# Last batch through the dense experts, the first three grouped with room for four steps of expert tiles

## The chip, the cores and the metric

One core of a Trainium2 chip runs the whole program. The metric is the device time of one execution in microseconds, taken as the median of several runs. All engine spans below come from one profiled execution.

## What is computed

Two layers over `x` of 4 batches, 256 tokens and 256 features, with a context of 4 x 256 x 64 beside it. Layer 0 builds an adjacency from the context (two projections, similarity, the top 76 of 256 in each row, a sigmoid, symmetrised), adds it and runs a gated feed-forward network with block-quantised operands. Layer 1 is an attention of 16 heads on low-rank keys, and then a mixture of 32 experts in which every token goes to one expert. The part that the change touches is that last one:

```python
logits = x4 @ router_w.T                     # 256 tokens, 32 experts
p = softmax(logits); e = argmax(p)           # one expert a token, weight p[e]
w_e = ternary(weight) * expert_masks[e]      # 256 x 256, values -1, 0, 1
out = x3 + p[e] * scale * (x4 @ w_e.T)       # x4 = layernorm(x3)
```

## The kernel before

The four batches are pipelined. In the pass of batch b the attention of batch b runs over eight head pairs p = 0 to 7. Beside it run the first layer of batch b + 1 (adjacency, top-k, feed-forward) and the experts of batch b - 1. The order on TensorE is a list written out by hand: `tensor_order()` places steps at four slots of a pair, `moe[p][0]` to `moe[p][3]`. Slot 0 stands after the key projections, slots 1 and 2 around `attn_turn(b, p, 0)` and the feed-forward steps, slot 3 just before `attn_turn(b, p, 1)`, and behind that come the scores of the next pair. The other engines walk the same list. PSUM has one large bank (QB) and six of 128x512 (S0, S1, QC, TP, GA, UA). A bank's `filled` and `drained` semaphores are counted over its turns in that list. S0 and S1 serve the scores and the experts, GA and UA the first layer.

The experts are *grouped*. `routing` finds each token's expert. `rank` and `tiles` (VectorE and TensorE) sort the tokens into 40 tiles of 32 slots, each tile belonging to one expert, and write the 40 expert numbers to `et`. `gather` (6 steps) permutes the tokens into the slots by matmuls with a 0/1 matrix, drained by ScalarE. `group` g (5 steps) multiplies 8 tiles by their 8 expert matrices: 32 matmuls into one bank (S0 for even g, S1 for odd g), drained by ScalarE into `osort[g % 2]`. The expert matrices lie as 8-bit floats in HBM (`wE_d`, 32 x 64 KB, written early in the program). `load_tiles(b, g)` fetches 8 of them, each with an address read from `et`, so SyncE executes 8 loads of 64 KB with a register load ahead of each. `wtile` holds two steps of 8 tiles, so the loads of step n wait until step n - 2 was multiplied. `store_sorted(b, g)` writes `osort` to HBM, `unsort(b)` on GpSimd fetches the 256 token rows back by an indirect DMA, and `result(b)` scales them, weights them and adds `x3`.

SyncE's queue is in order. Ahead of the first `load_tiles` stand the loads of x and context for batches 2 and 3. After that each batch is `load_tiles(0)`, `load_tiles(1)`, then `load_tiles(g)` and `store_sorted(g - 2)` in turn, the last two stores, and the store of the result. ScalarE drains `group` g only when the store of the step that used the same `osort` half has landed.

For the last batch nothing runs beside: after the attention of batch 3 the program goes through `att_out(3)`, the fourth layer norm, `moe_turn(3)`, `logits(3)`, `rank`, `tiles`, six gathers, five groups, `unsort` and `result`.

## Time and profile before

| | us |
|---|---|
| median of 3 runs | 685.72 (678.52 to 688.59) |
| the profiled execution | 686.24 |
| its span, first to last instruction | 684.4 |
| mean granted TensorE clock | 0.873 of 2.4 GHz |
| TensorE busy in the span | 501.1 (73%) |
| VectorE, ScalarE, GpSimd busy | 359.9, 228.3, 247.9 |

Busy time is the sum of an engine's own instructions. Start times in the rows below are counted from the first instruction of the span. A matmul's listed length is longer than its pitch, since successive ones overlap; the distance between two starts gives the pace.

### The profile page before, as it was taken

The numbers are of one execution on the slowest core, as the hardware profiler recorded it, in microseconds if no ns is written. First come the engines' busy times: TensorE is split into PE (matmuls) and PEld (weight loads), VectorE is DVE, ScalarE is ACT, GpSimd is POOL, SyncE is SP. The second block draws the span as 40 slices with busy tenths as digits, with TensorE's granted clock in tenths as the row PEclk, the third lists the DMA queues.
The fourth block names the chain that finished last, engine by engine and source line by source line (L and its number), as shares of the span: only waits on it lengthen the run. The fifth ranks groups of instructions, "written<-read, shape, count | busy, mean of one in ns | idle before, by whom it ended". The sixth has DMA issues, their size and how long they took to land.

```text
span 684.4 us, 9759 instructions
## 1 busy us (share of the span) xinstructions
PE 501.1 (73%) x3284; PEld 328.0 (48%) x3284; DVE 359.9 (53%) x711; ACT 228.3 (33%) x610; POOL 247.9 (36%) x258
## 2 busy tenths in 40 slices
PE   2863675877887698799987978998798986565211
PEld 1752244545445465555565645556475553351100
DVE  3999692587687238965643696476226321002000
ACT  1843121333323314363432336334114642303000
POOL 3765442368458512321344314123403220340003
PEclk9976898989999789999999999999799997866555
DMA  7941000034204300012310001121000212201222
GB/s 286 363 160 61 1 0 4 1 113 155 79 22 133 97 2 18 1 56 73 95 32 16 0 10 55 49 73 51 31 1 5 59 47 74 66 15 39 74 82 68
DMA packets 44416, 43.93 MB, mean 64 GB/s; under 512 B 7888, under 2 KB 40528, under 8 KB 43472
## 3 DMA queue, kind: packets, MB, share of 16 engines
q1 hardware_dynamic: 43984, 42.27, 19.3%
q0 software_dynamic: 384, 1.05, 0.5%
q8 instruction: 26, 0.43, 0.3%
q14 instruction: 22, 0.18, 0.1%
HBM read 34.92 MB, written 8.39 MB: 63 GB/s over the span
## 4 chain that ended last, share of the span: by engine, by line
PE 36%; DVE 26%; issue 11%; POOL 9%; SPq 7%; ACT 7%; DMA 2%; POOLq 0%; DVEq 0%; ACTq 0%
PE qc L560 9%; PE qb L560 8%; PE ga L560 6%; PE s L560 5%; SPq L521 4%; PE ua L560 3%; SPq L523 3%; PE tp L563 3%; DVE wk L1147 3%; POOL reg L1458 2%; DVE top L1145 2%; DVE amax L1072 2%; ACT reg L942 2%; POOL wst L1506 2%; DVE reg L1219 2%
## 5 line engine op out<-in xcount | busy, mean ns | idle before, releaser
L1458 POOL TENSOR_TENSOR reg<-reg,rsum 128x512 f32<-128x512 f32 x64 | 68.9, 1096 | 177.0 <-DVE rsum L1233 177.0
L942 ACT ACTIVATE reg<-s,nmax 128x256 f32<-128x256 f32 x128 | 58.9, 476 | 47.2 <-DVE nmax L1226 47.1
L560 PE MATMUL qc<-reg,wM 128*64 128x256 f32 (+1 forms) x384 | 71.1, 409 | 4.5 <-DVE reg L1219 2.8
L560 PE MATMUL qb<-reg,wA_hi 128*128 128x256 f16 x384 | 71.0, 291 | 2.7 <-ACT reg L927 2.7
L563 PE MATMUL tp<-idn,reg 128*128 128x128 f32 x248 | 43.9, 304 | 38.6 <-POOL reg L1458 21.6
L1226 DVE TENSOR_REDUCE nmax<-s 128x2 f32<-128x512 f32 x64 | 40.9, 680 | 34.6 <-PE s L560 34.6
L864 ACT COPY reg<-tp 128x512 f32<-128x512 f32 (+1 forms) x56 | 32.0, 571 | 81.1 <-PE tp L563 81.1
L1219 DVE TENSOR_TENSOR reg<-qb,cosq 128x768 f32<-128x768 f32 x32 | 30.5, 954 | 51.5 <-PE qb L560 51.5
L560 PE MATMUL s<-wtile,moe 128*32 128x256 fp8e4 x640 | 26.2, 317 | 42.0 <-DMA wtile<-wE_d 41.5
L563 PEld LDWEIGHTS tp<-idn,reg 128*128 128x128 f32 x248 | 30.9, 153 | 52.9 <-POOL reg L1458 28.1
L560 PEld LDWEIGHTS qc<-reg,wM 128*64 128x64 f32 (+1 forms) x384 | 38.2, 158 | 34.3 <-issue 22.2
L560 PEld LDWEIGHTS qb<-reg,wA_hi 128*128 128x128 f16 x384 | 36.2, 103 | 23.4 <-issue 12.7
L1506 POOL TENSOR_TENSOR wst<-masks,tern 128x512 fp8e4<-128x512 f32 x32 | 45.0, 1435 | 5.2 <-DMA masks<-in_moe_masks 5.2
L560 PEld LDWEIGHTS s<-wtile,moe 128*32 128x32 f16 x640 | 18.3, 109 | 49.1 <-issue 46.8
L560 PE MATMUL qb<-reg 128*64 128x256 f32 x256 | 37.3, 412 | 5.7 <-ACT reg L864 2.9
L560 PE MATMUL s<-reg 64*128 64x256 f32 x256 | 39.2, 427 | 1.8 <-ACT moe L864 1.5
L560 PE MATMUL qb<-reg,wA_lo 128*128 128x256 f16 x192 | 39.7, 291 | 0.0
L560 PE MATMUL ga<-wG,ffn 128*128 128x512 f32 x64 | 32.7, 636 | 9.5 <-DVE sg L1182 8.8
L560 PE MATMUL ga<-wD,ffn 128*128 128x256 f32 x128 | 34.5, 430 | 2.4 <-ACT ffn L864 2.4
L1389 POOL TENSOR_TENSOR ffn<-ffn,qsc 128x1024 f32<-128x1024 f32 (+1 forms) x12 | 19.5, 1623 | 42.1 <-DVE ffn L1096 42.1
L1384 POOL TENSOR_SCALAR small<-small 128x2 f32<-128x2 f32 x32 | 7.4, 232 | 68.3 <-DVE small L1122 66.5
L864 ACT COPY reg<-qb 128x256 f32<-128x256 f32 x32 | 11.9, 372 | 58.7 <-PE qb L560 58.7
(191 smaller groups left out, 959.8 us busy)
## 6 DMA issues: line engine op xcount, KB each, us to landing
wtile<-wE_d SPq DMA_DIRECT2D x160, 64.0 KB, 1.7
masks<-in_moe_masks SPq DMA_DIRECT2D x16, 512.0 KB, 3.7
y_d<-masks SPq DMA_DIRECT2D x20, 256.0 KB, 2.3
wM<-in_att_wq SPq DMA_DIRECT2D x1, 2048.0 KB, 8.5
moe<-in_wo_t SPq DMA_DIRECT2D x1, 2048.0 KB, 12.8
wE_d<-wst SPq DMA_DIRECT2D x16, 128.0 KB, 1.9
reg<-in_kc_q SPq DMA_DIRECT2D x1, 1536.0 KB, 11.7
reg<-in_qr_t SPq DMA_DIRECT2D x1, 1536.0 KB, 19.6
```

Of the source, the lines that this page charges most:

```text
L521: e = sp.value_load(et[0:1, 8 * g + i:8 * g + i + 1], min_val=0, max_val=E - 1)
L523: sp.dma_start(wtile[:, o:o + P], wE_d[bass.ds(e, 1)].rearrange("o p x -> p (o x)")).then_inc(ld_w[n % 2].sem, 16)
L560: return nc.tensor.matmul(dst, lhsT, rhs, start=start, stop=stop, skip_group_check=not check)
L563: return nc.tensor.transpose(dst, src, idn[:, :])
L864: nc.scalar.copy(dst, src).then_inc(bank.drained, 1)
L942: nc.scalar.activation(attn[p % 2][:, k * S:(k + 1) * S], s.tensor[:, (k % 2) * S:(k % 2 + 1) * S], ACT.Exp, bias=nmax[:, o:o + 1], accum_ ...
L1147: nc.vector.match_replace(wk[:, t * S:(t + 1) * S], best, cur, -3.0e38).then_inc(topk_step.sem, 1)
L1219: nc.vector.tensor_tensor(qcs[:, g * J * S:(g + 1) * J * S], QB.tensor[:, 0:J * S], tab[:, :], ALU.mult).then_inc(qc_ready.sem if g == 0 e ...
L1226: nc.vector.tensor_reduce(nmax[:, o:o + 2], v3(k.tensor[:, :], T), AX_X, ALU.max, negate=True).then_inc(nmax_ready.sem, 1)
L1389: nc.gpsimd.tensor_tensor(v3(dst, blocks), v3(src, blocks), scale.unsqueeze(2).to_broadcast([P, blocks, BLK]), ALU.mult).then_inc(ready.se ...
L1458: nc.gpsimd.tensor_tensor(a, a, rsum[:, o + 2 * hh:o + 2 * hh + 2].unsqueeze(2).to_broadcast([P, 2, S]), ALU.mult).then_inc(attn_ready.sem, 1)
L1506: last = nc.gpsimd.tensor_tensor(we[:, :, c, :], src[:, c], tern[:, c * D:(c + 1) * D].unsqueeze(1).to_broadcast([P, EC, D]), ALU.mult, sa ...
```

## The change

The last batch gets a *dense* form. All 32 expert matrices (2 MB) are fetched by one DMA into the space of the feed-forward weights `wG` and `wU`. Every token half t (0, 1) is multiplied by all 32 matrices: 16 fills of two banks, each bank two experts wide (128x512), even fills in GA and UA for tokens 0 to 127, odd ones in S0 and S1 for tokens 128 to 255. `selw` is the routing weight where the expert is the token's own, and 0 elsewhere. ScalarE drains the first half with a scale by `selw` (two instructions a bank) and GpSimd adds the drained rows up. VectorE drains the second half with a multiply-add straight from PSUM (two instructions a bank). At the end each path adds its two partial sums, multiplies by `scale` and adds `x3`, and each half is stored by its own DMA. The tokens are split in a high and a low 16-bit part from the transposed `x4T`, by ScalarE and VectorE, no longer by GpSimd.

For batches 0 to 2 `wtile` holds four steps of tiles instead of two; all five `load_tiles` of a batch are queued ahead of all five stores; the loads of x and context for batch 3 move behind the fourth `load_tiles` of batch 0; gathers and groups move to other slots; `unsort` moves behind the last `rstd` of the pass. The four new functions `expert` stand in the order TensorE, ScalarE, VectorE, GpSimd in the diff. To make room, `qm` now shares `sim` and `wk`, `wst` lies in `moe`, and the raw `wo` passes through `wtile`.

```diff
-    steps += [("att_out", B - 1), ("moe_turn", B - 1), ("logits", B - 1), ("rank", B - 1), ("tiles", B - 1)]
-    steps += [("gather", B - 1, i) for i in range(GATHERS)]
-    steps += [("group", B - 1, g) for g in range(GROUPS)]
+    steps += [("att_out", B - 1), ("moe_turn", B - 1), ("logits", B - 1)]
+    steps += [("expert", B - 1, f) for f in range(FILLS)]
...
-    ([("gather", 0)], [], [("gather", 1)], [("gather", 2)]),
-    ([("gather", 3)], [], [("gather", 4)], [("gather", 5)]),
-    ([("group", 0)], [], [("group", 1)], []),
-    ([("group", 2)], [], [("group", 3)], []),
-    ([("group", 4)], [], [], []),
+    ([], [("gather", 0)], [("gather", 1)], [("gather", 2)]),
+    ([("gather", 3)], [("gather", 4)], [], [("gather", 5)]),
+    ([], [], [], [("group", 0)]),
+    ([("group", 1)], [], [], [("group", 2)]),
+    ([("group", 3)], [], [], [("group", 4)]),
...
-                if n >= 2:
-                    key = ("group", (n - 2) // GROUPS, (n - 2) % GROUPS)
+                if n >= RING:
+                    key = ("group", (n - RING) // GROUPS, (n - RING) % GROUPS)
...
-            for b in range(2, B):
-                load_a(b)
-                load_b(b)
-            for b in range(B):
-                load_tiles(b, 0)
-                for g in range(1, GROUPS):
+            load_a(2)
+            load_b(2)
+            for b in range(B - 1):
+                for g in range(GROUPS):
                     load_tiles(b, g)
-                    if g >= 2:
-                        store_sorted(b, g - 2)
-                store_sorted(b, GROUPS - 2)
-                store_sorted(b, GROUPS - 1)
+                    if g == RING - 1 and b + 3 < B:
+                        load_a(b + 3)
+                        load_b(b + 3)
+                for g in range(GROUPS):
+                    store_sorted(b, g)
+                if b == B - 2:
+                    key = ("ffn_up", B - 1, 3)
+                    for k in both_banks(*key):
+                        sp.wait_ge(k.filled, k.done(key))
+                    sp.dma_start(v3(wE.bitcast(F32), E), wE_d[:, :, :].rearrange("e p x -> p e x")).then_inc(ld_dense.sem, 16)
...
+            def expert(b, f):
+                q, t = divmod(f, T)
...
+                for half, k in enumerate(both_banks("expert", b, f)):
+                    e = EF * q + 2 * half
+                    pe.wait_ge(k.drained, k.free(("expert", b, f)))
+                    for c in range(C):
+                        for i, src in enumerate((xhi, xlo)):
+                            last = mm(v3(k.tensor[:, :], 2), src[:, c * S + t * P:c * S + (t + 1) * P], w[:, e:e + 2, c, :],
+                                      c == 0 and i == 0, c == C - 1 and i == 1)
+                    last.then_inc(k.filled, 1)
...
+            def expert(m):
+                for half, k in enumerate(both_banks(*key)):
+                    n = 2 * m + half
+                    act.wait_ge(k.filled, k.done(key))
...
+                    if n > 2:
+                        act.wait_ge(summed.sem, n - 2)
+                    for i in range(2):
+                        e = EF * m + 2 * half + i
+                        dst = acc[:, 0, i] if n == 0 else scaled[half][:, i * D:(i + 1) * D]
+                        ins = nc.scalar.activation(dst, k.tensor[:, i * D:(i + 1) * D], ACT.Copy, scale=selw[:, 0, e:e + 1])
+                    ins.then_inc(k.drained, 1)
...
+            def expert(m):
+                for i in range(EF):
+                    e, chain, k = EF * m + i, i % 2, banks[i // 2]
+                    src, w = k.tensor[:, chain * D:(chain + 1) * D], selw[:, t, e:e + 1]
...
+                        ins = nc.vector.scalar_tensor_tensor(acc[:, t, chain], src, w, acc[:, t, chain], ALU.mult, ALU.add)
+                    ins.then_inc(acc_step.sem if chain == 0 else k.drained, 1)
...
+            def expert(m):
+                for half, k in enumerate(both_banks(*key)):
+                    n = 2 * m + half
+                    pool.wait_ge(k.drained, k.done(key))
+                    if n > 1:
+                        pool.wait_ge(summed.sem, n - 1)
+                    if n > 0:
+                        nc.gpsimd.tensor_tensor(acc_rows[:, 0:2 * D], acc_rows[:, 0:2 * D], scaled[half], ALU.add)\
+                            .then_inc(summed.sem, 1)
...
-                    if p == PAIRS - 1 and b >= 1:
-                        unsort(b - 1)
...
                 if b >= 1:
+                    unsort(b - 1)
                     result(b - 1)
```

## Rows read from the trace of the kernel before

**Rows 1.** Page of the profile, part 2: TensorE and its clock in 40 slices

```profile
PE   2863675877887698799987978998798986565211
PEclk9976898989999789999999999999799997866555
```

**Rows 2.** Timeline of the end: start, length, instruction, count, idle before and its cause

```profile
614.07 1.91 PE L560 MATMUL qc<-rtr,moe 128*128 128x32 f32 x8 [0.68 <-ACT moe L864]
616.02 0.23 DVE L1251 TENSOR_REDUCE small<-qc 128x2 f32<-128x64 f32 x1 [6.70 <-PE qc L560]
617.44 0.17 DVE L1264 RECIPROCAL small<-small 128x2 f32<-128x2 f32 x1
...
621.10 25.82 SPq L523 DMA_DIRECT2D wtile<-wE_d  x24
...
667.24 1.90 PE L560 MATMUL s<-wtile,moe 128*32 128x256 fp8e4 x32 [7.27 <-DMA wtile<-wE_d]
...
676.94 1.26 POOL L1490 TENSOR_TENSOR tern<-tern,scl 128x512 f32<-128x512 f32 x1 [1.78 <-DMA tern<-y_d,slot_u]
...
681.52 0.38 SPq L553 DMA_DIRECT2D out<-tern  x1
```

**Rows 3.** Busy time by stretch: stretch, length, busy of each engine, clock, DMA share, GB/s

```profile
624.00:628.00 4.00, 3.74 (x14) 0.80 (x14) 0.00 (x0) 3.59 (x8) 0.00 (x0) 1.00 0.19 55
628.00:684.00 56.00, 9.49 (x160) 6.29 (x160) 0.00 (x0) 3.42 (x6) 6.40 (x6) 0.52 0.24 74
```

**Rows 4.** Timeline of batch 3's attention, where batch 2 is grouped

```profile
527.88 0.18 DVE L1305 TENSOR_SCALAR et<-qc 1x40 int32<-1x40 f32 x1
...
528.78 33.67 SPq L523 DMA_DIRECT2D wtile<-wE_d  x24
...
554.18 8.27 SPq L523 DMA_DIRECT2D wtile<-wE_d  x8
...
563.72 8.30 SPq L523 DMA_DIRECT2D wtile<-wE_d  x8
...
573.59 1.90 PE L560 MATMUL s<-wtile,moe 128*32 128x256 fp8e4 x32 [6.71 <-DMA wtile<-wE_d]
...
576.46 2.08 PE L560 MATMUL s<-reg 64*128 64x256 f32 x8
```

**Rows 5.** DMA issues: size of each, median us from issue to landing

```profile
y_d<-masks SPq DMA_DIRECT2D x20, 256.0 KB, 2.3
wM<-in_att_wq SPq DMA_DIRECT2D x1, 2048.0 KB, 8.5
```

**Rows 6.** Timeline, matmul pace at 2.4 GHz (two pairs), weight load at 1.2 GHz

```profile
531.87 0.53 PE L560 MATMUL s<-moe,xhi 128*128 128x432 f16 x2
532.23 0.53 PE L560 MATMUL s<-moe,xlo 128*128 128x432 f16 x2
...
620.60 0.15 PEld L560 LDWEIGHTS s<-moe,xlo 128*128 128x128 f16 x1 [0.21 <-issue]
```

**Rows 7.** Timeline, prices of the drains and adds

```profile
550.44 0.47 ACT L942 ACTIVATE reg<-s,nmax 128x256 f32<-128x256 f32 x1
550.89 0.48 ACT L942 ACTIVATE reg<-s,nmax 128x256 f32<-128x256 f32 x1
...
359.53 0.42 DVE L1196 TENSOR_TENSOR x<-y,ga 128x256 f32<-128x256 f32 x1 [7.00 <-PE ga L560]
...
678.30 1.84 POOL L1493 TENSOR_SCALAR tern<-tern,small 128x256 f32<-128x256 f32 x2
680.23 1.26 POOL L1495 TENSOR_TENSOR tern<-tern,reg 128x512 f32<-128x512 f32 x1
...
213.97 7.81 POOL L1506 TENSOR_TENSOR wst<-masks,tern 128x512 fp8e4<-128x512 f32 x4
```

**Rows 8.** Timeline of batches 1 and 2, around the groups and `result`

```profile
442.45 0.44 SPq L528 DMA_DIRECT2D y_d<-masks  x1
...
455.57 1.06 PE L560 MATMUL s<-wtile,moe 128*32 128x256 fp8e4 x32
...
362.47 0.20 POOL L1409 TENSOR_TENSOR small<-small 128x2 f32<-128x2 f32 x1
...
374.55 1.50 POOL L1384 TENSOR_SCALAR th<-th 128x512 f32<-128x512 f32 x1 [7.37 <-ACT th L908]
```

More of the change, by code:

```diff
@@ L30 @@
 NEC = E // EC
+EF = 4
 G = 32
+RING = 4
 NT = 40
@@ L224, in banks_of @@
         return [("GA", "UA")[args[1] % 2]]
+    if name == "expert":
+        return ("GA", "UA") if args[1] % T == 0 else ("S0", "S1")
     if name == "group":
@@ L294, in build @@
         top = sb("top", T * 8)
-        ffn = sb("ffn", 6144)
-        hid, qy, qm, hq = (ffn[:, i * I:(i + 1) * I] for i in range(4))
-        hqT = ffn[:, 4096:5120]
-        xn = ffn[:, 5120:5632]
-        xqT = ffn[:, 5632:6144]
+        ffn = sb("ffn", 5120)
+        hid, qy, hq = (ffn[:, i * I:(i + 1) * I] for i in range(3))
+        qm = simwk[:, :]
+        hqT = ffn[:, 3072:4096]
+        xn = ffn[:, 4096:4608]
+        xqT = ffn[:, 4608:5120]
+        acc = ffn[:, 0:T * 2 * D].rearrange("p (t k d) -> p t k d", t=T, k=2)
+        acc_rows = ffn[:, 0:T * 2 * D]
+        scaled = [ffn[:, 1024:1536], ffn[:, 1536:2048]]
+        selw = v3(ffn[:, 2048:2048 + T * E], T)
         sg = sb("sg", 512)
@@ L396, in build @@
         st_w = [count(f"st_w{i}", 0, 16 * NEC // 2) for i in range(2)]
-        ld_w = [count(f"ld_w{i}", 0) for i in range(2)]
-        st_y = [count(f"st_y{i}", 16 * (GROUPS + 1 - i) // 2 if i == 0 else 16 * (GROUPS // 2)) for i in range(2)]
+        ld_w = [count(f"ld_w{i}", 0) for i in range(RING)]
+        ld_dense = count("ld_dense", 0, 16)
+        st_y = [count(f"st_y{i}", 16 * ((GROUPS + 1 - i) // 2)) for i in range(2)]
         ld_y = count("ld_y", 16 * T)
@@ L853, in _ @@
                 keys_turn, x_turn, project_first, project, to_keys, scores, attn_turn, context, att_out, moe_turn, logits, rank, tiles,
-                gather, group)}
+                gather, group, expert)}
             for name, *args in order:
@@ L952, in moe_turn @@
                 drain(TP, ("moe_turn", b), x4T, TP.tensor[:, :])
+                if b == B - 1:
+                    act.wait_ge(TP.drained, TP.done(("moe_turn", b)))
+                    nc.scalar.copy(xhi[:, :], x4T).then_inc(xsplit_ready.sem, 1)
             def route_exp(b):
@@ L961, in gather @@
                 c, (o, w) = i // len(PIECES), PIECES[i % len(PIECES)]
+                if b == 0 and i == 0:
+                    for q in st_w:
+                        act.wait_ge(q.sem, q.setup)
                 for h, k in enumerate(both_banks(*key)):
@@ L972, in group @@
                 drain(bank_of("group", b, g), ("group", b, g), osort[g % 2], bank_of("group", b, g).tensor[:, :])
+            def expert(m):
+                key = ("expert", B - 1, T * m)
+                for half, k in enumerate(both_banks(*key)):
+                    n = 2 * m + half
+                    act.wait_ge(k.filled, k.done(key))
+                    if m == 0 and half == 0:
+                        act.wait_ge(rt_step.sem, rt_step.at(B - 1, 6))
+                    if n > 2:
[5 more added lines that the diff above has]
+                    ins.then_inc(k.drained, 1)
             def moe_step(b, name, *args):
@@ L1057, in _ @@
             route_exp(B - 1)
-            for i in range(GATHERS):
-                gather(B - 1, i)
-            for g in range(GROUPS):
-                group(B - 1, g)
+            for m in range(FILLS // T):
+                expert(m)
         @block.vector
@@ L1375, in _ @@
             routing(B - 1)
-            rank(B - 1)
-            tiles(B - 1)
+            dve.wait_ge(rt_step.sem, rt_step.at(B - 1, 6))
+            for m in range(FILLS // T):
+                expert(m)
+            o, last = acc[:, 1, 0], ("expert", B - 1, FILLS - 1)
+            k = both_banks(*last)[1]
+            dve.wait_ge(k.drained, k.done(last))
+            dve.wait_ge(acc_step.sem, 2 * FILLS // T)
+            nc.vector.tensor_tensor(o, o, acc[:, 1, 1], ALU.add).then_inc(last_step.sem, 1)
+            dve.wait_ge(last_step.sem, 1)
+            nc.vector.tensor_tensor(o, o, scl[:, :], ALU.mult).then_inc(last_step.sem, 1)
+            dve.wait_ge(last_step.sem, 2)
+            nc.vector.tensor_tensor(o, o, x3[:, D:2 * D], ALU.add).then_inc(last_step.sem, 1)
         @block.gpsimd
@@ L1565, in _ @@
                 if b >= 1:
+                    unsort(b - 1)
                     result(b - 1)
             rstd(B - 1, 3)
-            split(B - 1)
-            unsort(B - 1)
-            result(B - 1)
+            for m in range(FILLS // T):
+                expert(m)
+            o, last = acc[:, 0, 0], ("expert", B - 1, FILLS - T)
+            k = both_banks(*last)[1]
+            pool.wait_ge(k.drained, k.done(last))
+            pool.wait_ge(summed.sem, FILLS - 1)
+            nc.gpsimd.tensor_tensor(o, o, acc[:, 0, 1], ALU.add).then_inc(osum.sem, 1)
+            pool.wait_ge(osum.sem, 1)
+            nc.gpsimd.tensor_tensor(o, o, scl[:, :], ALU.mult).then_inc(half_step.sem, 1)
+            pool.wait_ge(half_step.sem, 1)
+            nc.gpsimd.tensor_tensor(o, o, x3[:, 0:D], ALU.add).then_inc(o_ready.sem, 1)
 def tables():
```

85 lines of the change are left out of this document (65 added, 20 removed).

## The prediction, made before the changed kernel was run

> **What bounds the kernel now.** I read the page's slices first [rows 1]: TensorE is busy in 60 to 99% of most slices at nearly full clock, until slice 34; in the last four it is busy in 10 to 20%, at half clock. The end is therefore a stretch with another limit, and the timeline of the end says which [rows 2]. The logits of the last batch are done at 616.0, and the span ends at 684.4: 68.4 us for the experts of one batch. In that time SyncE issues 40 loads of 64 KB; 24 of them take 25.82 us, so one step of 8 costs 8.6 us of issue, and each group of TensorE work (1.90 us) waits for them, the last one for 7.27 us. The windows confirm it [rows 3]: of 56 us TensorE works 9.5, all other engines less, and the DMA engines are only 24% busy. What is late is SyncE's issue of dynamic loads, not bandwidth and not arithmetic. Behind it come the sort's store, the indirect fetch, and `result`.
>
> The same limit shows once more in the attention of batch 3, which has nothing of a next batch to fill it [rows 4]. `et` of batch 2 is written at 527.9, SyncE starts at 528.8, but the third step of loads starts only at 554.2, when group 0 has freed its half of `wtile`. Group 3 then waits 6.71 us for its tiles, and the scores of pair 6 start at 576.46, half clock by then.
>
> **Part 1, the dense last batch.** Counted from 616.0.
>
> TensorE: 16 fills x 2 banks x 4 matmuls = 128 matmuls of 512 columns. At the full clock two matmuls of 432 columns start 0.36 us apart from the next two [rows 6], 0.42 ns a column, so 0.213 us for 512. The trace has no 8-bit operand on the full array, only the groups' 32-column tiles; I allow up to 8% over the pace, 0.23 us. With 0.221: 28.3 us (27.3 to 29.4). The clock is at 1.2 GHz when the logits end. After comparable starts it rose inside a few us, and in the gathers it stayed at 1.00 although each step waited for a drain [rows 3]. I take 3 us of work at half clock, 1.5 us lost (0 to 3). TensorE ends at 616.0 + 28.3 + 1.5 = 645.8.
>
> Do the drains keep up? At full clock a step of four banks takes TensorE 3.5 us. ScalarE has four instructions in it; the pitch of its 128x256 reads from PSUM with a per-row operand is 0.45 us [rows 7], so 1.8 us. VectorE has four, a 128x256 from PSUM costs 0.42 [rows 7]: 1.7 us. GpSimd has two adds of 128x512 at 1.26 plus 0.08 [rows 7]: 2.7 us. Each is under 3.5, and a bank has three other fills' time for its drain. `selw` is ready at about 617.9 (the reciprocal at 617.44 [rows 2] and one small product); the first bank is full at about 617.8, so nothing waits. The split of `x4T` lies beside the logits. `rank`, `tiles`, gathers, groups, the store and the indirect fetch go.
>
> After TensorE's end: the last bank of the first half is full two fills earlier, 644.0; ScalarE is done with it at 645.1; GpSimd's last two adds end at 646.8; its three closing operations on 128x256 cost about 0.65 each by half of the 1.26 (one row has 0.92 for a scaled 256 [rows 7], an upper end), with gaps 2.2: 649.0. VectorE closes at about 648.2. Two stores are issued, the second at 649.5. From the issue of the result's store to the end of the span it is 684.4 - 681.52 = 2.9 us now [rows 2], so the span would end at 652.4. From the logits on: 36.4 us instead of 68.4, a gain of 32.0.
>
> The dense load of 2 MB must be there by 616. SyncE reaches it behind the last store of batch 2, about 585. A load of this size from HBM took 8.5 us [rows 5], in longer rows; by the 74 GB/s at 24% of the engines [rows 3], which is about 310 GB/s for this mix at full share, it takes 7 us. Even 20 us would be covered by the 30 in between. It runs beside the indirect fetch of batch 2, whose `result` ended 4 us ahead of its reader; I cost it at nothing, 0 to 3 us if the fetch queues behind it.
>
> **Part 2, batch 3's attention.** With room for four steps, loads 0 to 3 need no group, and load 4 only group 0, long done. SyncE issues all five in a row: 528.8 + 5 x 8.6 = 571.8. So no group waits for tiles: group 2 stands at slot 3 of pair 5, about 564.5, with its tiles there since 556. But the stores now stand behind all loads. Store 0 is issued at 571.8 and lands 2.3 us later [rows 5] at 574.3, and ScalarE may drain group 2 (same half of `osort`) only then. Behind that drain in ScalarE's queue stand the turned attention and the next pair; and S0 is held, which the scores of pair 6 need. So the wait of 6.71 us for tiles is replaced by one of about 8.5 us for a store. Scores of pair 6: 574.3 + 0.1 + 0.58 for the drain = 575.1, against 576.46. The pair that follows keeps its length less the small wait of the old group 4, and holds one group more, in slots with slack. Gain 1.3 us (0.5 to 2.5).
>
> **Part 3, batches 1 and 2.** The moves take groups out of the path before the scores of pair 6 (three stand there instead of four, 1.0 us each [rows 8]), and add two hand-overs of S0 just ahead of scores, about 0.25 each. I take 0.5 us gain a batch, 1.0 in all (from -1 to 2). The same store wait is covered here: in batch 2 the first three steps end at 442.4 [rows 8] after a start at 407, so load 4 follows group 0 (at about 442.5) and ends near 451; store 0 has landed by 453.5, and group 2 stands behind the last `ffn_up`, near 458: 4 to 5 us to spare. `unsort` moved behind `rstd` makes `result` end about 5 us later, near 372 in batch 1; GpSimd's next work starts at 374.55 [rows 8], so it hides, with 2 to 3 us of cover. The later load of batch 3's inputs is not read for some 40 us more. The shared buffers add no wait: the same engine uses them in order.
>
> **Sum.** 32.0 + 1.3 + 1.0 = 34.3 us. The profiled execution took 686.24, of which 684.4 is the span, and that lies 0.5 over the median: 651.9 by the profiled run, 651.4 by the median. Forecast 652, its own range 646 to 658: 1.5 for the pace of the matmuls, 1.5 for the clock, 2 for the parts 2 and 3, and the runs themselves, which spread from 678.5 to 688.6.
>
> **Rivals.**
> (a) *GpSimd bounds the dense stretch.* Its four products of 128x512 at 213.97 took 7.81 us beside VectorE work, 1.95 each instead of 1.26 [rows 7]. With 2.02 a step, 15 adds from 620.5 end at 650.8, the closing operations at 654, the span at 657.5: 657. For it: VectorE works all through. Against it: it reads one operand from PSUM, as it did in many stretches where GpSimd kept its pace. 0.12. The Trainium skill ("VectorE: DVE Perf Modes", section "Two Vector instructions with no wait between them") has the second SBUF read shared with GpSimd for Vector instructions of two SBUF tensors or in a two-port mode; by that rule the new multiply-add leaves GpSimd alone and this case falls away.
> (b) *TensorE does not keep its clock.* The fills go round four banks and each waits for a drain; if the gaps bring the clock down again for half of the stretch, 128 matmuls take 28.3 x 1.5 = 42 us and the time is 664; at 1.2 GHz throughout, 55 us, 677. The tail of the groups did run at 0.52 [rows 3], but with waits of 7 us; the gathers, with waits of 0.4, kept 1.00. 0.10. The Trainium skill ("TensorE: Matmul & The Clock Gate", section "A second HAM failure mode: psum-queue depth-cycling") reports just this for matmuls of 512 columns that cycle through PSUM banks. By that rule the time is near 664; by the gathers' row, 652.
> (c) *The wait for the store does not form*, because SyncE gets through its five steps sooner or group 2 comes later. Then all of the old wait goes: scores of pair 6 near 567, 643.5. Against it: both 8.6 us a step and the position of the store are plain. 0.10.
> (d) *Slower.* Each expert matmul stays at 1.2 GHz and shows its weight load: 0.427 + 0.15 [rows 6] = 0.577 us, 128 of them 73.9 us, the end at 616.0 + 73.9 + 6.6 less 2.3 = 694, a time of 696. It decides from (68.4 - 6.6 + 2.3) / 128 = 0.50 us a matmul. Against it: weight loads lay beside matmuls everywhere in the trace. 0.03.
>
> **How the numbers follow.** Forecast 0.65, (a) 0.12, (b) 0.10, (c) 0.10, (d) 0.03. The range reaches into (c) and to the first form of (b): 643 to 665. A measurement of this kernel tells about 2% from no change, 13.7 us: under 672 is faster. That is all but the full form of (b) and (d): faster 0.92, same 0.05, slower 0.03.
>
> **What would show it.** Right: no run of 40 tile loads at the end; about 30 us between the logits and TensorE's last matmul at a granted clock near 1.00, spacing 0.21 to 0.23; GpSimd finishing last; in batch 3 no group waiting for tiles, but ScalarE idle some 8 us before the third drain into `osort`, released by the landing of a store. Wrong: a clock of 0.5 to 0.8 in the stretch, GpSimd's adds longer than 1.7 us, TensorE waiting for the dense load, `att_out` of batch 3 late behind `result`, or a new wait in batches 1 and 2 at group 2.

## The result, and the profile after

The changed kernel takes 653.00 us (median of 4 runs, 652.87 to 654.12); the kernel before, taken on the same chip among them, 683.14 (4 runs, 678.52 to 688.59). The ratio is 0.956, with a 95% interval of 0.948 to 0.964. The profiled execution took 652.87 us with a span of 651.1, against 686.24 and 684.4: 33.3 us less.

The page's slices of the kernel after, TensorE and its granted clock in tenths, answer to [rows 1]:

```profile
PE   2871875868897689789997797899968989666696
PEclk9987699797999879989999898999987999976799
```

Where the kernel before was busy in 10 to 20% of its last three slices at half clock, there is now one slice busy to 90% or more and one to 60%, since TensorE ends at 644.7 of 651.1 us, both at nearly full clock. The slices cannot give the size, so all traces of this study are cut at three marks, which every kernel here has: `et` of batch 2 is written; VectorE's first reduction over the logits of batch 3 starts; the span ends.

| execution | `et` of batch 0 at | `et(0)` to `et(2)` | `et(2)` to logits | logits to end | span |
|---|---|---|---|---|---|
| before | 281.8 | 246.1 | 88.1 | 68.4 | 684.4 |
| after | 280.9 | 246.1 | 87.9 | 36.2 | 651.1 |

Of 33.3 us, 32.2 lie in the last stretch, 0.2 in batch 3's attention, none in batches 1 and 2, and 0.9 in the first pass, which the change leaves alone. That last number is within the spread of executions: in the twelve profiled ones of this study the first pass ends anywhere from 277.5 to 283.0. So times of whole executions are not compared to a microsecond here; the stretches are.

The end, in the timeline of the kernel after (start, length, engine, line, operation, idle time before and its releaser), answers to [rows 2]:

```profile
612.90 1.92 PE L590 MATMUL qc<-rtr,moe 128*128 128x32 f32 x8 [0.68 <-ACT moe L909]
...
614.63 0.61 PE L590 MATMUL ga<-wGU,xhi 128*128 128x512 fp8e4 x1
...
614.86 0.23 DVE L1319 TENSOR_REDUCE small<-qc 128x2 f32<-128x64 f32 x1 [0.64 <-PE qc L590]
...
618.88 0.59 PE L590 MATMUL s<-wGU,xhi 128*128 128x512 fp8e4 x1
...
619.30 0.38 PE L590 MATMUL s<-wGU,xlo 128*128 128x512 fp8e4 x1
...
619.52 0.38 PE L590 MATMUL s<-wGU,xhi 128*128 128x512 fp8e4 x1
...
643.08 2.67 POOL L1617 TENSOR_TENSOR ffn<-ffn 128x512 f32<-128x512 f32 x2 [0.77 <-ACT ffn L1038]
...
644.34 0.38 PE L590 MATMUL s<-wGU,xlo 128*128 128x512 fp8e4 x1
...
645.89 0.78 POOL L1696 TENSOR_TENSOR ffn<-ffn 128x256 f32<-128x256 f32 x1
...
648.42 0.35 SPq L580 DMA_DIRECT2D out<-ffn  x1
648.82 0.43 SPq L582 DMA_DIRECT2D out<-ffn  x1
```

The first eleven expert matmuls start 0.425 us apart, at 1.2 GHz; from 619.30 on the distance is 0.216. None waits. GpSimd's three closing operations take 0.78 us each; only the first is shown. The windows give the stretch as a whole (busy time and instructions of each engine, granted clock, DMA share, GB/s), where [rows 3] showed TensorE 9.5 us busy in 56:

```profile
614.60:644.60 30.00, 30.00 (x130) 13.00 (x129) 14.44 (x38) 13.67 (x33) 17.84 (x15) 0.92 0.00 1
```

TensorE is the only engine without a gap; GpSimd, the next, works 17.8 of 30 us. Batch 3's attention, which answers to [rows 4]:

```profile
527.88 43.72 SPq L543 DMA_DIRECT2D wtile<-wE_d  x40
...
562.49 1.06 PE L590 MATMUL s<-wtile,moe 128*32 128x256 fp8e4 x32
...
571.63 13.40 SPq L549 DMA_DIRECT2D y_d<-masks  x5
...
573.95 0.58 ACT L909 COPY masks<-s 128x512 f32<-128x512 f32 x1 [10.77 <-DMA y_d<-masks]
...
574.63 2.08 PE L590 MATMUL s<-reg 64*128 64x256 f32 x8 [10.50 <-issue]
...
585.25 0.82 SPq L576 DMA_DIRECT2D wGU<-wE_d  x1
...
598.09 1.26 POOL L1601 TENSOR_TENSOR tern<-tern,scl 128x512 f32<-128x512 f32 x1 [3.97 <-DMA tern<-y_d,slot_u]
```

All 40 loads go out in one piece of 43.7 us (1.09 each). Group 2 is computed at 562.5 to 563.5, and ScalarE then stands 10.77 us before its drain, until store 0, issued behind the last load, has landed. The scores of pair 6, whose bank that drain frees, start at 574.63: the "issue" before them is this wait seen from TensorE.

### The profile page after: what moved, and what is told of

It is laid out like the page before. It is cut to its first block, busy times and chain, and to the rows that moved or that the text cites. A ratio compares the mean times of both kernels' runs of the same rounds, so it can differ in the third digit from the quotient of the medians.

```text
span 651.1 us, 9473 instructions
## 1 busy us (share of the span) xinstructions
PE 508.7 (78%) x3221; PEld 329.7 (51%) x3221; DVE 376.3 (58%) x737; ACT 232.3 (36%) x626; POOL 261.7 (40%) x268
## 4 chain that ended last, share of the span: by engine, by line
PE 45%; DVE 24%; issue 11%; POOL 9%; ACT 8%; DMA 1%; SPq 0%; POOLq 0%; DVEq 0%; ACTq 0%
PE qc L590 11%; PE qb L590 10%; PE ga L590 8%; PE s L590 8%; PE ua L590 4%; PE tp L593 3%; DVE simwk L1212 3%; POOL reg L1569 2%; DVE top L1210 2%; ACT moe L909 2%; POOL moe L1629 2%; ACT reg L987 2%; DVE reg L1284 2%; DVE amax L1137 1%; DVE small L1184 1%
## 5 line engine op out<-in xcount | busy, mean ns | idle before, releaser
L987 ACT ACTIVATE reg<-s,nmax 128x256 f32<-128x256 f32 x128 | 58.9, 476 | 44.0 <-DVE nmax L1291 43.7
L1629 POOL TENSOR_TENSOR moe<-masks,tern 128x512 fp8e4<-128x512 f32 x32 | 45.5, 1449 | 5.2 <-DMA masks<-in_moe_masks 5.2
L590 PE MATMUL ga<-wGU,ffn 128*128 128x512 f32 x64 | 32.5, 632 | 8.5 <-DVE sg L1247 7.3
L590 PEld LDWEIGHTS s<-reg 64*128 64x128 f32 x256 | 24.6, 198 | 21.9 <-issue 20.8
L590 PE MATMUL ga<-wD,ffn 128*128 128x256 f32 x128 | 32.3, 410 | 2.4 <-ACT ffn L909 2.4
L590 PE MATMUL qc<-wF,reg 128*128 128x256 f32 x128 | 31.2, 407 | 0.5 <-ACT reg L909 0.5
```

Of the source, the lines that this page charges most:

```text
L590: return nc.tensor.matmul(dst, lhsT, rhs, start=start, stop=stop, skip_group_check=not check)
L987: nc.scalar.activation(attn[p % 2][:, k * S:(k + 1) * S], s.tensor[:, (k % 2) * S:(k % 2 + 1) * S], ACT.Exp, bias=nmax[:, o:o + 1], accum_ ...
L1629: last = nc.gpsimd.tensor_tensor(we[:, :, c, :], src[:, c], tern[:, c * D:(c + 1) * D].unsqueeze(1).to_broadcast([P, EC, D]), ALU.mult, sa ...
```

## The experiments

The theory on record: the dense end gives the gain, bounded by TensorE; the new queue order gives nearly nothing, because a wait for tiles turned into a wait for a store; GpSimd and the clock are near, but not bounds. The stretches below are those of this table: one profiled execution of each kernel. Where nothing was edited they repeat to 0.1 us from `et(2)` to the logits (87.9 to 88.0) and to 0.6 us in the dense end (35.6 to 36.2), but from `et(0)` to `et(2)` they spread by 11 us. The extra adds, the extra matmuls, the moved group 4 and the two together ran on one chip, the others on another, so their medians are compared by the ratio to the kernel before on the same chip.

| execution | `et(0)` at | to `et(2)` | to logits | to end | span | median | ratio to before |
|---|---|---|---|---|---|---|---|
| dense end alone | 278.7 | 244.9 | 87.7 | 36.0 | 647.4 | 652.08 | 0.953 (0.948 to 0.959) |
| ring and order alone | 277.5 | 247.8 | 88.0 | 69.1 | 682.4 | 686.25 | 1.004 (1.000 to 1.008) |
| store 0 ahead | 282.0 | 246.1 | 78.9 | 35.6 | 642.6 | 644.91 | 0.942 (0.937 to 0.947) |
| without low part | 281.8 | 246.1 | 87.9 | 30.0 | 645.8 | 647.56, one run | |
| 16 extra VectorE adds | 280.7 | 252.8 | 88.0 | 38.4 | 659.8 | 661.56, one run | |
| extra matmuls | 282.7 | 245.8 | 86.8 | 34.3 | 649.6 | 650.64 | 0.955 (0.950 to 0.960) |
| stores between, group 4 moved | 278.5 | 245.6 | 75.3 | 35.9 | 635.2 | 637.36 | 0.934 (0.929 to 0.938) |
| the two together | 278.3 | 241.5 | 74.9 | 35.7 | 630.3 | 635.22 | 0.931 (0.927 to 0.935) |
| and early dense load | 280.1 | 242.6 | 71.6 | 36.0 | 630.3 | 633.14 | 0.922 (0.916 to 0.929) |
| early dense load alone | 283.0 | 247.9 | 88.0 | 36.2 | 655.0 | 653.42 | 0.951 (0.946 to 0.956) |

**Dense end alone.** The changed kernel with two steps of tiles, the old queue and the old slots.

```diff
-RING = 4
+RING = 2
...
             for b in range(B - 1):
-                for g in range(GROUPS):
+                load_tiles(b, 0)
+                for g in range(1, GROUPS):
                     load_tiles(b, g)
...
-                for g in range(GROUPS):
-                    store_sorted(b, g)
+                    if g >= 2:
+                        store_sorted(b, g - 2)
+                store_sorted(b, GROUPS - 2)
+                store_sorted(b, GROUPS - 1)
```

> The dense last batch alone: two steps of tiles in the ring, the old order of SyncE's queue and the old slots of gathers and groups; the load of all matrices stays behind the stores of batch 2. Theory (the dense end is nearly the whole gain, the other two parts give 1 us together): 654 to 656, the end from the logits unchanged at 36.2 us, the old waits for tiles in batch 3 back. Rival (the new ring and order are worth several us): 658 or more.

Measured: 652.08 (649.23 to 655.92), 36.0 us from the logits to the end. The waits of TensorE for tiles are back in batch 3 (three, 8.1 us together, the longest 5.1), and that stretch still has 87.7 us against 87.9. The whole gain that these runs can tell is in this part of the change; the other gains nothing in that stretch, where 1 to 2 us were expected, and this kernel's median is even 0.9 us under that of the changed one.

**Ring and order alone.** Four steps of room, all loads ahead of all stores, the new slots, and the last batch grouped.

```diff
-    steps += [("att_out", B - 1), ("moe_turn", B - 1), ("logits", B - 1)]
-    steps += [("expert", B - 1, f) for f in range(FILLS)]
+    steps += [("att_out", B - 1), ("moe_turn", B - 1), ("logits", B - 1), ("rank", B - 1), ("tiles", B - 1)]
+    steps += [("gather", B - 1, i) for i in range(GATHERS)]
+    steps += [("group", B - 1, g) for g in range(GROUPS)]
...
```

> The new ring, queue order and slots alone, the last batch grouped again as before. Theory: 683 to 686 by the profiled span, that is the kernel before less 1 to 2 us, since SyncE's 40 loads at 1.08 us bound the end whatever the room: from the logits to the end 66 to 71 us; the stores behind all loads may add up to 2 us there. Rival (room in the ring speeds up the grouped end, because loads no longer wait for groups): 5 or more us less than before.

Measured: 686.25 (10 runs), ratio 1.0042 with an interval just above one. The 1 to 2 us did not come. At the end all 40 loads stand ahead of the first store here too. Two of the last groups still wait for their tiles, since SyncE's issue of 43.6 us bounds them whatever the room, and the last one waits for a ScalarE drain that stands behind the store (TensorE rows of this kernel):

```profile
645.74 1.90 PE L578 MATMUL s<-wtile,moe 128*32 128x256 fp8e4 x32 [6.77 <-DMA wtile<-wE_d]
654.97 1.90 PE L578 MATMUL s<-wtile,moe 128*32 128x256 fp8e4 x32 [7.33 <-DMA wtile<-wE_d]
665.00 1.90 PE L578 MATMUL s<-wtile,moe 128*32 128x256 fp8e4 x32 [8.13 <-ACT masks L897]
```

**Store 0 ahead.** One line moved in SyncE's queue of the changed kernel: the store of step 0 before the fifth step of loads.

```diff
-                    if g == RING - 1 and b + 3 < B:
-                        load_a(b + 3)
-                        load_b(b + 3)
-                for g in range(GROUPS):
+                    if g == RING - 1:
+                        if b + 3 < B:
+                            load_a(b + 3)
+                            load_b(b + 3)
+                        store_sorted(b, 0)
+                for g in range(1, GROUPS):
                     store_sorted(b, g)
```

> The changed kernel, with the store of step 0 queued ahead of the fifth step of tile loads instead of behind it. Theory (the wait of 10.77 us in batch 3 is SyncE's order): the store is issued at about 563, as soon as the fourth step of loads is out, and lands near 565.2; ScalarE waits about 2 us instead of 10.8, the scores of pair 6 start near 566 instead of 574.6, and the time is 8 to 9 us less than 653, about 644.5. Rival (something else in that pair is late just behind it, such as the fifth step of tiles): group 4 then waits for its tiles, whose loads end near 572.5 in either order, and no more than 2 to 4 us are gained, 650.

Measured: from `et(2)` to the logits 78.9 us instead of 87.9, time 644.91. ScalarE's drains of the groups in the timeline of this kernel:

```profile
566.72 0.58 ACT L911 COPY masks<-s 128x512 f32<-128x512 f32 x1 [2.43 <-DMA y_d<-masks]
...
575.94 0.58 ACT L911 COPY masks<-s 128x512 f32<-128x512 f32 x1 [3.80 <-DMA y_d<-masks]
```

10.77 us of waiting became 2.43. The store behind the loads was worth 9 us of critical path: that is shown. Against the kernel with two steps of room (87.7 us), the room and the new slots pay 8.8 us with the store moved and nothing without it; no run parts the room from the slots.

**Without the low part.** Left out: the product with `xlo`, so TensorE has 64 of 128 matmuls and the result only the f16 precision of `x4`.

```diff
-                        for i, src in enumerate((xhi, xlo)):
+                        for i, src in enumerate((xhi,)):
                             last = mm(v3(k.tensor[:, :], 2), src[:, c * S + t * P:c * S + (t + 1) * P], w[:, e:e + 2, c, :],
-                                      c == 0 and i == 0, c == C - 1 and i == 1)
+                                      c == 0 and i == 0, c == C - 1 and i == 0)
```

> The changed kernel without the low 16-bit part of the tokens in the dense matmuls, so 64 matmuls instead of 128 (this part of the result is left out). Theory (TensorE bounds the dense stretch, GpSimd comes next with 15 adds at 1.34 us): TensorE's own 27.6 us halve, but GpSimd's adds then follow one another and the stretch shrinks by only 6 to 8 us, 645 to 647. Rival (TensorE alone counts): 13 to 14 us less, 639. Rival (GpSimd or a drain bounds it already): no more than 2 us less, 651.

Measured, in one execution: the end 30.0 us instead of 36.2. GpSimd's rows now are one nearly unbroken run, 1.40 a step of addition:

```profile
619.47 1.27 POOL L1617 TENSOR_TENSOR ffn<-ffn 128x512 f32<-128x512 f32 x1 [8.63 <-ACT ffn L1038]
621.00 19.56 POOL L1617 TENSOR_TENSOR ffn<-ffn 128x512 f32<-128x512 f32 x14 [0.27 <-ACT ffn L1038]
640.70 0.73 POOL L1696 TENSOR_TENSOR ffn<-ffn 128x256 f32<-128x256 f32 x1
```

Halving TensorE's work gained 6.2 us and not 14: TensorE is the bound of the dense stretch, and GpSimd is next, 6 us behind.

**Sixteen extra VectorE adds.** A 128x512 addition of two SBUF tiles behind every second multiply-add, its result unused.

```diff
+                    if i % 2 == 1:
+                        if 2 * m + i // 2 > 0:
+                            dve.wait_ge(extra.sem, 2 * m + i // 2)
+                        nc.vector.tensor_tensor(th[:, :], x2[0][:, :], x2[1][:, :], ALU.add).then_inc(extra.sem, 1)
```

> The changed kernel with 16 extra VectorE additions of 128x512 in the dense stretch, each of two inputs in SBUF (the sum is read by nobody), one behind each bank that VectorE has drained. Alone such an addition takes 0.69 us, so VectorE would work 3.1 us in a step of 3.45 and nothing would be late. Theory (GpSimd was spared only because VectorE's multiply-add reads one input from PSUM): GpSimd's adds rise from 1.27 to 1.6 us or more where they meet the extra ones, and so do these, VectorE passes 3.45 us a step, and the end moves by 3 to 7 us: from the logits 39 to 43 us instead of 36.2. Rival (no contention between the two on such instructions): all lengths as before, from the logits 36 to 37 us.

Measured, in one execution: the end 38.4 us, 2.1 more and between the two expectations. (6.7 us of this run's 661.56 are a long pass of batches 1 and 2, where nothing was edited.) The groups of instructions in the end stretch of this kernel (line, engine, operation, count, busy us, mean ns, idle before):

```profile
L1622 POOL TENSOR_TENSOR ffn<-ffn 128x512 f32<-128x512 f32 x15 | 20.7, 1381 | 16.2 <-ACT ffn L1039 15.1
L1410 DVE TENSOR_TENSOR th<-x,x 128x512 f32<-128x512 f32 x16 | 17.4, 1087 | 0.0
L1405 DVE SCALAR_TENSOR_TENSOR ffn<-s,ffn 128x256 f32<-128x256 f32 x30 | 13.0, 472 | 0.5 <-PE s L591 0.5
...
L1489 DVE TENSOR_TENSOR ffn<-ffn 128x256 f32<-128x256 f32 x1 | 0.9, 939 | 0.0
L1491 DVE TENSOR_TENSOR ffn<-ffn,scl 128x256 f32<-128x256 f32 x1 | 0.4, 426 | 0.0
```

And those of the kernel after:

```profile
L1617 POOL TENSOR_TENSOR ffn<-ffn 128x512 f32<-128x512 f32 x15 | 19.0, 1266 | 16.9 <-ACT ffn L1038 15.9
L1404 DVE SCALAR_TENSOR_TENSOR ffn<-s,ffn 128x256 f32<-128x256 f32 x30 | 13.0, 479 | 12.0 <-PE s L590 12.0
...
L1486 DVE TENSOR_TENSOR ffn<-ffn,scl 128x256 f32<-128x256 f32 x1 | 0.8, 828 | 0.0
L1484 DVE TENSOR_TENSOR ffn<-ffn 128x256 f32<-128x256 f32 x1 | 0.4, 424 | 0.0
```

The multiply-add that reads PSUM costs the same in both (472, 479 ns) and leaves GpSimd's addition at 1.27 us, the 1.26 of [rows 7]. Additions of two SBUF tiles do collide with GpSimd: the extra ones take 0.68 us where GpSimd is idle (the first two), 1.09 in the mean and up to 1.77, while GpSimd's own go from 1.27 to 1.38. The price fell mostly on VectorE; the 1.6 us expected of GpSimd's additions did not come. The same shows unprompted in VectorE's closing operations on 128x256. In the kernel after, the first takes 0.42 us, with GpSimd at work in about half of it, and the two that lie wholly beside GpSimd's take 0.83 each. In the run with extra adds it is the other way round: 0.94 for the first, beside GpSimd's last operation, and 0.43 and 0.42 after GpSimd has ended. The Trainium skill ("VectorE: DVE Perf Modes", "Two Vector instructions with no wait between them") has the second SBUF read shared with GpSimd; the trace agrees on which instructions collide.

The 2.1 us came by VectorE. From 629.8 us on it has work without a wait, 32.3 of the 38.4 us in all, and a step takes 3.6 us instead of 3.45. At 0.68 us for each extra add a step of VectorE would be 3.1 us and fit; at 1.09 it does not. GpSimd still waits before each step.

**Extra matmuls.** 36 products of 256 columns into the free bank GA behind `att_out(3)`, results unused, to keep TensorE busy while the fourth layer norm runs.

```diff
+            def warm(n):
+                pe.wait_ge(GA.drained, GA.free(("expert", B - 1, 0)))
+                for _ in range(n):
+                    mm(GA.tensor[:, 0:S], wA_hi[:, 0:P], wA_hi[:, 0:S])
...
+                if b == B - 1:
+                    warm(36)
```

> The changed kernel with 36 extra matmuls of 256 columns (their result is read by nobody) right behind the attention's output product of batch 3, where TensorE is idle for 4.7 us. Theory (the dense stretch starts at 1.2 GHz because of that idle time, and this costs 2.3 us of the 30): TensorE stays at 2.4 GHz through the transpose and the logits (1.12 and 1.92 us become 0.66 and 0.98) and from the first expert matmul on, 3.5 us less in all, 649.5. Rival (the clock is back down whatever is run there, or the extra matmuls delay the transpose): 653 or more.

Measured in TensorE's rows:

```profile
607.85 4.09 PE L590 MATMUL ga<-wA_hi 128*128 128x256 f16 x36
612.69 0.66 PE L593 MATMUL tp<-idn,reg 128*128 128x128 f32 x4 [0.75 <-ACT reg L952]
614.02 1.08 PE L590 MATMUL qc<-rtr,moe 128*128 128x32 f32 x8 [0.67 <-ACT moe L916]
615.44 0.38 PE L590 MATMUL ga<-wGU,xhi 128*128 128x512 fp8e4 x1 [0.34 <-issue]
```

The turn takes 0.66 us instead of 1.12, the logits 1.08 instead of 1.92, and all expert matmuls run at 2.4 GHz. The stretches are 1.1 and 1.9 us shorter, 3.0 in all where 3.5 was expected. By the medians alone (650.64 against 653.00) this could not be told from chance; the stretches of this one profiled execution carry it. The 1.9 us are not to be had every time: the kernel with the early dense load, further below, has the same extra matmuls in the same place, and its first eight expert matmuls ran at 1.2 GHz.

**Stores between the loads, group 4 moved.** Queue: loads 0, 1, 2, store 0, load 3, store 1, load 4, the other stores; group 4 from slot 3 of pair 6 to slot 0 of pair 7.

```diff
+                    if 2 <= g < RING:
+                        store_sorted(b, g - 2)
-                for g in range(GROUPS):
+                for g in range(RING - 2, GROUPS):
                     store_sorted(b, g)
...
-    ([("group", 3)], [], [], [("group", 4)]),
-    ([], [], [], []),
+    ([("group", 3)], [], [], []),
+    ([("group", 4)], [], [], []),
```

> As the run with the store of step 0 first, and further: the stores of steps 0 and 1 behind the third and fourth loads, and group 4 one slot later, at the start of pair 7. In the last run batch 3 still had three waits, of 2.4 us for the store of step 0, 1.3 us for the tiles of step 4, and 3.8 us of ScalarE for the store of step 1. Theory (they are SyncE's 40 issues of 1.08 us again, not TensorE work): all three shrink to under 1 us and batch 3 from the tile numbers to the logits takes 75 to 77 us instead of 78.9, the time is 641 to 643. Rival (attention itself is the bound there): 78 us or more, 645.

Measured: 75.3 us from `et(2)` to the logits, 12.6 less than in the kernel after; time 637.36, better than expected. Of the 7.4 us by which this span is shorter than that with store 0 ahead, 3.6 are in this stretch; 4.0 lie before `et(2)`, which these edits hardly touch, and are within the spread there. The run does not part the two stores from the slot of group 4. ScalarE no longer waits for any store. But `result(2)` has caught up with the output product, which ends at 590.64, and releases `x3` 0.3 us later:

```profile
579.10 0.95 POOL L1594 DMA_INDIRECT tern<-y_d,slot_u  x1 [0.30 <-issue]
...
581.11 9.53 PE L592 MATMUL qc<-wF,reg 128*128 128x256 f32 x32 [0.52 <-ACT reg L911]
...
586.28 1.26 POOL L1603 TENSOR_TENSOR tern<-tern,scl 128x512 f32<-128x512 f32 x1 [6.24 <-DMA tern<-y_d,slot_u]
...
590.96 0.69 DVE L1305 TENSOR_TENSOR reg<-x,qc 128x512 f32<-128x512 f32 x1 [16.86 <-POOL tern L1608]
```

The indirect fetch lands 6.24 us after the end of its second issue, beside the dense load of 2 MB, issued at 575.3.

**The two together:** the extra matmuls (`warm(n)`) and the new order, with 26 more ahead of the turn of pair 7.

```diff
+                if (b, p, hh) == (B - 1, PAIRS - 1, 0):
+                    warm(26)
...
+                if b == B - 1:
+                    warm(36)
```

> The two previous edits together, and 26 more extra matmuls ahead of the last turned attention of batch 3, so that the output product (32 matmuls, 10.03 us) starts at 2.4 GHz too: 7.1 us by its length in batch 2. Theory (all these gains stand in one chain and add up): 9 to 12 for the queue order and slots, 3.5 for the clock behind the product, 2 to 3 for the product, so 635 to 638. Rival (they overlap, since the extra matmuls only fill time in which something else is waited for): 641 or more.

Measured: 635.22, in the range that was expected, but by luck. It is 2 us under the one before and within its interval, and in the profiled executions 4.1 of the 4.9 us between the two lie in batches 1 and 2, where the two kernels are the same. From `et(2)` on only 0.6 us were gained:

```profile
581.67 1.26 POOL L1612 TENSOR_TENSOR tern<-tern,scl 128x512 f32<-128x512 f32 x1 [5.79 <-DMA tern<-y_d,slot_u]
...
586.35 0.69 DVE L1314 TENSOR_TENSOR reg<-x,qc 128x512 f32<-128x512 f32 x1 [16.55 <-POOL tern L1617]
...
590.99 1.01 PE L595 MATMUL tp<-idn,reg 128*128 128x128 f32 x4 [3.07 <-ACT reg L956]
```

The product takes 7.17 us instead of 9.53 and ends at 584.0, 64.2 us after `et(2)` instead of 66.5. But `x3` starts at 586.35, released by `result(2)`, and TensorE, idle for 3.07 us, makes most of the turn and all of the logits (1.92 us) at 1.2 GHz again. A step made faster in front of a wait gave nearly nothing: the rival on record, that these gains overlap, was right.

**Early dense load.** The load moved from behind the stores of batch 2 to ahead of its tile loads, in two kernels: in the one just described, and alone in the kernel after.

```diff
             for b in range(B - 1):
+                if b == B - 2:
+                    key = ("ffn_up", B - 1, 3)
+                    for k in both_banks(*key):
+                        sp.wait_ge(k.filled, k.done(key))
+                    sp.dma_start(v3(wE.bitcast(F32), E), wE_d[:, :, :].rearrange("e p x -> p e x")).then_inc(ld_dense.sem, 16)
                 for g in range(GROUPS):
                     load_tiles(b, g)
...
-                if b == B - 2:
-                    key = ("ffn_up", B - 1, 3)
...
```

> Everything in the run before with stores between the loads, group 4 moved and extra matmuls, and the dense load moved: SyncE issues it before the loads of batch 2's tiles, when the gate/up weights have long been used, so that batch 2's indirect fetch has the queue to itself. There, the fetch (issued 573.5 and 574.9) landed 5.79 us after the second issue, result(2) was done at 586.25, and x3 waited for it 2.5 us past the end of the output product (583.85). Theory (the dense load beside the fetch delays it): the wait of the GpSimd multiplication for the fetch falls from 5.8 to under 3 us, result(2) is done by 583.5, x3 starts at the product's end, so 2.3 us less, and since TensorE then idles 1 us and not 3 before the transpose, logits may run at 2.4 GHz, 0.5 to 0.9 more: from et(2) to the logits 72 us in place of 74.9, time 629 to 633 for runs at the middle of the other's (635.2). Rival (the fetch is slow by itself: 512-byte rows, addressed one by one): the wait stays above 5 us and nothing changes, 75 us. Rival on the slower side (the 2 MB load now stands ahead of the loads of batch 2's tiles, 8.5 us at most): only if it is issued late, after 511; expected at or before 500.

> The changed kernel with the dense load alone moved ahead of the loads of batch 2's tiles. There result(2) was done 3.8 us before the output product of batch 3 ended, so by the prediction's reading the contention costs nothing: wait of GpSimd for the fetch from 3.97 to under 2.5 us, time unchanged within 0.5 us (from et(2) to the logits 87.9, end 36.2). Rival (the dense load beside batch 3's last pair also slows something else, such as the attention weights' or the indirect issue): 1 to 2 us less.

Measured in the first, SyncE, GpSimd, VectorE and TensorE:

```profile
492.64 0.82 SPq L569 DMA_DIRECT2D wGU<-wE_d  x1
...
577.87 0.95 POOL L1603 DMA_INDIRECT tern<-y_d,slot_u  x1 [0.30 <-issue]
580.63 1.26 POOL L1612 TENSOR_TENSOR tern<-tern,scl 128x512 f32<-128x512 f32 x1 [1.81 <-DMA tern<-y_d,slot_u]
...
587.07 0.69 DVE L1314 TENSOR_TENSOR reg<-x,qc 128x512 f32<-128x512 f32 x1 [14.37 <-PE qc L592]
...
593.04 1.08 PE L592 MATMUL qc<-rtr,moe 128*128 128x32 f32 x8 [0.67 <-ACT moe L920]
...
594.70 0.63 PE L592 MATMUL ga<-wGU,xlo 128*128 128x512 fp8e4 x1
...
598.09 0.38 PE L592 MATMUL s<-wGU,xlo 128*128 128x512 fp8e4 x1
```

The wait for the fetch fell from 5.79 to 1.81 us, `x3` is released by the product again, the logits run at 2.4 GHz, and the stretch has 71.6 us instead of 74.9: the contention is shown. Of these 3.3 us, 2.2 are the earlier start of `x3` and 1.1 the clock behind it. The clock then fell all the same: from 594.70 to 598.09 the expert matmuls start 0.425 us apart, as in the kernel without extra matmuls, and the end has 36.0 us, not the 34.3 of the run with extra matmuls alone. TensorE did the same just before in both (36 matmuls of 4.09 us, idle 0.75, the turn, idle 0.67, the logits, idle 0.35), so these rows do not say what decides it. Alone in the kernel after, the stretches stayed at 88.0 and 36.2: there it was covered, as the prediction had costed it. The wait for the fetch is 2.53 us there instead of 3.97, but this fall says little: with no load beside it the same fetch left GpSimd waiting 3.00 us in the kernel before and 2.23 in that with ring and order alone, and with the load issued as early ahead of it as in the kernel after, 1.91 us in that with store 0 ahead. With 633.14 us (ratio 0.922, 0.916 to 0.929) the first has the lowest median of the study, though its interval overlaps that of the two together. It is 3% under the changed kernel with the early load alone, on the same chip (653.42, against 653.00 for the changed kernel itself).

## Why the prediction was right

The forecast was 652; the changed kernel's median is 653.0. That it is so close is partly luck: the three parts were forecast at 34.3 us and gave 32.4 in the stretches, 0.9 us came back in the first pass, and single executions of the kernel before spread over 10 us. By its steps:

- **Which stretch bounds.** The slices of [rows 1] show 10 to 20% in the last three and not four; the fourth from the end, at 50%, has the gathers. The reading of the limit stands. 68.4 us from the logits on were forecast as 36.4 and measured as 36.2. The kernel with the dense end alone has the whole gain.
- **TensorE's time.** Forecast 28.3 + 1.5. Measured 30.0: the pace was 0.216 us, not 0.221 (128 x 0.216 = 27.6), and eleven matmuls at 1.2 GHz cost 11 x 0.21 = 2.3. Two small errors cancel.
- **Drains.** A step takes 3.45 us; GpSimd needs 2.67 of it, VectorE 1.74, ScalarE 4 x 0.42 = 1.7. Forecast 2.7, 1.7, 1.8. Nothing waits for a drain. (A bank has the time of the three other banks for its drain, not of three fills, and the last bank of the first half is full one fill before the end, not two; the numbers worked out from it, 1.8 us before TensorE's end, are those of one fill.)
- **The tail.** Forecast 6.6 us from TensorE's last matmul to the end of the span; 6.5 measured. Here too errors cancel. GpSimd's last addition ends 1.2 us behind TensorE's end instead of 1.0, and the closing operations take 2.6 us instead of 2.2, 0.78 each and not 0.65; but from the issue of the last store to the end of the span it is 2.3 us instead of 2.9.
- **The dense load** is issued at 585.25 as forecast and no one waits for it; from issue to landing it takes 10.2 us, not the 7 to 8.5 worked out, all of it covered. Costing its contention with the indirect fetch at nothing was right as long as other waits held the path up: with the store wait gone it puts `result(2)` 0.3 us behind the output product, and with the product made 2.4 us shorter as well it is worth 3.3 us.
- **Part 2's mechanism** came as described: store 0 issued at 571.63 (forecast 571.8), landed by 573.95, scores of pair 6 at 574.63 (forecast 575.1). ScalarE's wait is 10.77 us, not 8.5, for group 2 was done 1 us earlier after `et(2)` than worked out, and the wait is counted from ScalarE's drain before. The size of the gain was off: 0.2 us instead of 1.3. Scores of pair 6 are 0.9 us earlier after `et(2)` (47.7 against 48.6), since the five steps of loads took 43.7 us and not 43.0. (By its own terms the sum is 571.8 + 2.3 = 574.1, not 574.3, and the gain there 1.7.) From there to the scores of pair 7 it is 10.1 us instead of 9.7, and from the output product to the logits 16.5 instead of 16.3. The term left out is the clock behind the longer wait: the 8 matmuls into `qb` behind these scores take 1.90 us instead of 1.45 (1.09 at full clock, as in pair 7), and the output product 10.03 instead of 9.80. "Holds one group more, in slots with slack" held only because of a wait: from the next matmuls to the scores of pair 7 it is 6.28 us with two groups and 6.30 before with one group and the 1.18 us that it waited for its tiles. The pair had no other slack, and the end of that wait gave nothing.
- **Part 3** was forecast at 1.0 us and measured at 0.0 (246.1 in both); executions of the study spread in this stretch from 241.5 to 252.8, with nothing edited there beyond the order of SyncE's queue and the slots, so neither 1 us nor its absence can be shown. The run of ring and order alone (247.8, ratio 1.004) speaks against a gain.
- **Rivals.** (a) *GpSimd as the bound* is refuted, its additions stayed at 1.27 us; even with VectorE work on two SBUF tiles beside them they rose to 1.38 only, where (a) needs about 2, and it was VectorE that became late. (b) *The clock*: 0.92 granted in the stretch, the loss all at its start. The Trainium skill's rule ("TensorE: Matmul & The Clock Gate", "A second HAM failure mode: psum-queue depth-cycling") would have made it near 664. This trace does not agree: 512-column matmuls went round four banks 0.216 us apart, with no gap between banks and no fall of the clock once it had risen. (c) *No store wait* did not happen by itself, but making it happen gave 644.9 with store 0 moved, near the 643.5 that (c) put on it, and 637.4 with a finer order. (d) *Slower*: the weight loads lie beside the matmuls, 13.0 us of them inside 30.0.

## What to carry to other kernels

When one queue issues both loads that run ahead and stores that others wait for, more room for loads moves the wait to the first store; put each store right where its data is ready, and only then does the room pay (9 us for one line here). After a bound falls, look again at what had been costed at nothing because something else covered it: the 2 MB load beside an indirect fetch cost 0 us at first and 3.3 us after two other waits had been taken away. Moving it some 80 us earlier cost nothing in the stretches from `et(2)` on; whether it costs something in batches 1 and 2 is not shown, since executions there spread over 11 us. Where executions differ by more than the effect, cut the traces at marks that all kernels share and compare stretches.

## What the runs showed of the hardware

- A matmul of 512 columns with an 8-bit moving operand and an f16 stationary one is paced at 0.216 us at 2.4 GHz and 0.425 at 1.2, its weight load hidden (13.0 us of loads inside the 30.0).
- With 36 useless matmuls of 4.09 us in the gap, the turn and the logits behind it ran at 2.4 GHz in both kernels where TensorE was then idle for 0.75 us; after 4.68 us idle (kernel after) and 3.07 us idle (the two together) the logits ran at 1.2 GHz. What comes next is not settled by it: in one of the two kernels all expert matmuls ran at 2.4 GHz, in the other the clock fell behind the logits and eight of them ran at 1.2.
- A load of 64 KB whose address comes from a register costs 1.0 to 1.1 us of SyncE's issue (40 in 43.72 us; 8 in 7.95 us at the least); it lands in 1.8 us.
- VectorE and GpSimd slow each other where VectorE adds two SBUF tiles: 128x256 from 0.42 to 0.83 us, 128x512 from 0.68 to 1.09 in the mean. A multiply-add with one PSUM operand does not slow GpSimd's additions (1.27 us), and two of them take 0.87 us with GpSimd idle or at work.
- Two indirect fetches of 128 rows of 1 KB land 1.8 to 3.0 us after the end of the second issue with no load beside them. With a 2 MB load issued some 4 us ahead of the second, 5.8 and 6.2; with it issued 8 to 9 us ahead, when most of its 10 us are over, 1.9 to 4.0.
